# Second cross attention, selection: a text mask added by products over 128 rows of the array

## What is computed

```python
Q = (x_text @ Wq).reshape(Bb, Tt, H, DH)          # H = 4 heads, DH = 32
K = (x_vision @ Wk).reshape(Bb, Gg, H, DH)        # Gg = 4096
scores = jnp.einsum('bthd,bghd->bhtg', Q, K) / np.sqrt(DH).astype(np.float32)
scores = jnp.where(mask[:, None, None, :], scores, -jnp.inf)
topv, topi = jax.lax.top_k(scores, K_TOP)         # K_TOP = 32
probs = jax.nn.softmax(topv, axis=-1)
attn = jnp.zeros_like(scores).at[bi, hi, ti, topi].set(probs)
attn_mean = attn.mean(axis=1)
```

## Time and profile before

| | us |
|---|---|
| median of 3 runs | 2346.48 (2339.76 to 2350.98) |
| the profiled execution | 2345.02 |
| its span, first to last instruction | 2343.2 |
| TensorE busy, share of the span | 1861.1, 79% |
| VectorE busy | 1253.5, 53% |
| ScalarE busy | 1029.8, 44% |
| mean granted clock of TensorE | 0.854 |

### The profile page before, as it was taken

The page is one execution under the profiler, slowest core; times in us unless marked ns, Lnnn a source line. Parts: engine busy times, 40 slices in busy tenths (PEclk is TensorE's granted clock), DMA queues, the critical chain, the costliest instruction groups (busy, mean ns, idle before and its releaser), DMA issues.

```text
span 2343.2 us, 34857 instructions
## 1 busy us (share of the span) xinstructions
PE 1861.1 (79%) x13676; PEld 1136.0 (48%) x13676; DVE 1253.5 (53%) x3081; ACT 1029.8 (44%) x1381; POOL 769.4 (33%) x685
## 2 busy tenths in 40 slices
PE   5879999999999988886878687876877376766775
PEld 2434544454454445654664244544544355454553
DVE  5143332424233103556764859979789934636575
ACT  1357567657766871122212435455455211013452
POOL 6244334414432300001200457857678221310000
PEclk7989999999999999998886556777777698778887
DMA  6656557555553600002000011312211340000000
GB/s 139 126 102 117 114 117 120 119 116 107 114 118 88 114 39 1 2 2 92 27 2 12 14 55 48 88 50 60 82 48 55 106 152 1 0 1 1 1 5 14
DMA packets 78046, 150.27 MB, mean 64 GB/s; under 512 B 15464, under 2 KB 63144, under 8 KB 71464
## 3 DMA queue, kind: packets, MB, share of 16 engines
q1 hardware_dynamic: 64304, 102.06, 15.5%
q0 software_dynamic: 12768, 42.59, 11.8%
q10 hardware_dynamic: 792, 3.17, 0.3%
HBM read 93.85 MB, written 2.62 MB: 41 GB/s over the span
## 4 chain that ended last, share of the span: by engine, by line
PE 51%; DVE 25%; ACT 12%; issue 6%; DMA 4%; POOL 3%; DVEq 0%; ACTq 0%; POOLq 0%; SPq 0%
PE R L112 32%; PE B L112 17%; ACT P L571 6%; DVE PM L1700 6%; DVE CA L1658 4%; POOL KST L789 2%; DMA KST<-OV 2%; ACT PM L1585 2%; PE B L178 2%; DVE CA L1670 1%; DVE T L1672 1%; ACT PS L2253 1%; DVE RT L604 1%; DMA CT<-in_ctxT 1%; ACT RT L116 1%
## 5 line engine op out<-in xcount | busy, mean ns | idle before, releaser
L571 ACT ACTIVATE P<-R 128x1024 f32<-128x1024 f32 x512 | 506.9, 1026 | 217.6 <-PE R L112 182.6
L112 PE MATMUL R<-QS,KST 100*128 100x256 bf16 x2048 | 295.5, 276 | 61.8 <-ACT P L571 54.2
L112 PEld LDWEIGHTS R<-QS,KST 100*128 100x128 bf16 x2048 | 169.2, 98 | 225.5 <-ACT P L571 121.8
L116 ACT ACTIVATE SC<-R 128x1024 f32<-128x1024 f32 x128 | 129.6, 1024 | 240.3 <-PE R L112 129.5
L1658 DVE MAX8 CA<-SC 128x8 f32<-128x128 f32 x1024 | 203.2, 277 | 15.7 <-ACT SC L116 14.8
L200 POOL TENSOR_TENSOR LNrs<-LNve,pk_const 128x2 f32<-128x2 f32 x36 | 25.4, 705 | 521.5 <-DVE LNve L196 521.4
L112 PE MATMUL R<-OV,QT 32*128 32x512 f32 x512 | 190.9, 834 | 0.0
L1773 POOL TENSOR_TENSOR ACC<-ACC,PM 128x4096 f32<-128x4096 f32 x21 | 186.2, 8867 | 1.7
L1700 DVE SCALAR_TENSOR_TENSOR PM<-SC,T,PM 128x4096 f32<-128x4096 f32 x32 | 149.7, 4713 | 41.0 <-ACT AT L116 21.0
L789 POOL DMA_DIRECT2D KST<-OV x300 | 145.1, 492 | 73.8 <-PE R L112 56.4
L112 PE MATMUL R<-P,VP 128*32 128x256 f32 x2304 | 154.8, 385 | 1.0 <-ACT P L571 1.0
(11 more groups left out here) (364 smaller groups left out, 3407.3 us busy)
## 6 DMA issues: line engine op xcount, KB each, us to landing
KST<-OV POOLq DMA_DIRECT2D x276, 128.0 KB, 10.8
CT<-in_ctxP SPq DMA_DIRECT2D x40, 768.0 KB, 4.4
CN<-in_ctxn SPq DMA_DIRECT2D x64, 384.0 KB, 3.4
CT<-in_ctxT SPq DMA_DIRECT2D x64, 192.0 KB, 2.4
KST<-OV SPq DMA_DIRECT2D x84, 128.0 KB, 10.9
KST<-in_ctxP ACTq DMA_DIRECT2D x4, 768.0 KB, 9.1
QS<-x_q POOLq DMA_DIRECT2D x24, 128.0 KB, 5.5
pk_a<-in_pk_a SPq DMA_DIRECT2D x1, 3014.0 KB, 17.8
```

The source lines that it names most:

```text
L112: return e.matmul(o, l, r, start=st, stop=sp, skip_group_check=True)
L116: return e.activation(o, i, ACT.Copy)
L571: e.activation(P[(32 * p + k0) % 3][:, :], ring.at(("s", p, k0))[:, :], ACT.Exp).then_inc(*EX.up((p, k0)))
```

## The change

The mask is added by products over all 128 rows of the array: `ONB` is now zero but for its first row of ones, and `MRT` has the mask's row on partition 0 and zeros on the 127 others. The zeros are written once, by GpSimd, at the start of `stage_moe`. `ONB` takes two memsets and a wait between them. The mask's row goes to one partition, by one DMA in place of four. The number of products, what they write and their order remain.

```diff
@@ stage_moe, gpsimd
             def gpsimd(e):
+                e.memset(OV[:, NK:NK + NK // 2], 0.0)
                 for i in range(2):
                     ins = e.memset(LT[i][:, :], 0.0)
@@ stage_x1a, tensor, scores
                     for n in range(2):
-                        r = 32 * (2 * hp + n)
-                        mm(e, ps[:, n * 512:n * 512 + 512], ONB[r:r + 1, :], MRT[r:r + 1, cs], True, False)
+                        mm(e, ps[:, n * 512:n * 512 + 512], ONB[:, :], MRT[:, cs], True, False)
@@ stage_x1a, vector
                 e.memset(ON1[:, :], 1.0).then_inc(*QV.up())
-                e.memset(ONB[:, :], 1.0).then_inc(*QV.up("ones"))
+                e.memset(ONB[:, :], 0.0).then_inc(*QV.up())
+                e.wait_ge(*QV.now())
+                e.memset(ONB[0:1, :], 1.0).then_inc(*QV.up("ones"))
@@ stage_x1a, sync, mask_rows
-                    for h in range(4):
-                        e.dma_start(MRT[32 * h:32 * h + 1, :].rearrange("o (a k) -> o a k", k=128), MR[:, :]).then_inc(*MRD.up(b if h == 3 else None))
+                    e.dma_start(MRT[0:1, :].rearrange("o (a k) -> o a k", k=128), MR[:, :]).then_inc(*MRD.up(b))
```

## The result

| | before | changed |
|---|---|---|
| median of 4 runs, us | 2343.99 (2339.76 to 2350.98) | 2375.39 (2368.75 to 2381.61) |
| profiled execution, us | 2345.02 | 2371.99 |
| span, us | 2343.2 | 2370.2 |
| mean granted clock | 0.854 | 0.870 |

The changed kernel is slower: ratio 1.0131, 95% interval 1.0089 to 1.0172. The forecast was 2373 us.

A forecast was written before the change was run, and what follows sets the result against it. TensorE's chunks were taken to set the time in ten of 16 places, VectorE coming last in six. Batch 0 +10.0, eight places +12.8 and five +5 gave +27.8 us on 2345.0: 2373 us, range 2342 to 2402.

The forecast's parts named there:

- The second pass: Mask pair on TensorE: two 128-row products can't run side by side; +0.43 us a chunk at half clock, +0.21 at full.
- The change-over: Each chunk on TensorE: going from 128 rows to 32 and back costs 0.20 us, bounds 0 and 0.41.
- Places 0 and 1: First 16 chunks (a place: two heads, 128 queries, eight chunks): +2.4 us with the clock rising in place 1, +10.1 without.
- The sign named for it: Place 1: if the clock stays 0.50 behind the query product, the zero rows don't count.
- Place 2: Third place of batch 0: two chunks wait ready in the ring, six follow at half clock; +3.8 us.
- Place 3: Fourth place of batch 0, with the next batch's keys between chunks, at half clock; +3.8 us, chunks of about 6.6.
- The third rival: Full-row mask alone holds full clock from the first chunks; -21 us, 2324 us; place 3 chunks under 5 us; chance 0.18.
- That rows of zeros count for the clock: New masks on TensorE: full-row products count for raising the clock though 127 rows hold zeros.
- the rival of 2393 us: The clock doesn't react to zero rows in the new masks; +48 us, 2393 us; chance 0.22.
- The rest: Later places: eight waiting for ScalarE at 1.6 us each, +12.8; five with VectorE last at 1 each, +5.
- The smaller edits at nothing: GpSimd memset, ONB's second memset and wait, and single mask DMA: 0 us; DMA gain at most 1.8 us three times.

The follow-up runs named there:

- e2: Kernel before with each pair of one-row mask products issued twice, no change-over and no full rows; 2376.75 us, ratio 1.0132.
- e5: Kernel before with one product of 128 rows and a single column ahead of each one-row mask pair; 2368.66 us, ratio 1.0081.
- e3: Changed kernel with ones in place of zeros in the mask's 127 lower rows, weights there still zero; 2379.85 us, ratio 1.0143 to the kernel before.
- e1: Kernel before with mask products of 32 rows (one of mask, 31 of zeros) in each head's own strip, new memset included; 2348.28 us, ratio 1.0004.
- e7: Kernel before with idle 128-row products at the stage's start (36) and behind the second chunk of five places; 2328.28 us, ratio 0.9909.
- e8: Kernel before with 32-row masks in own strips, idle 128-row products at the stage's start, in five places and ahead of place 3; 2331.37 us, ratio 0.9895.
- e6: Kernel before with 36 idle 128-row products at the stage's start, while TensorE waits; one-row masks stay; 2347.72 us, ratio 0.9981.
- e9: Kernel before with 32-row masks in each head's own strip and 36 idle 128-row products at the stage's start; 2339.87 us, ratio 0.9943.

## Why the prediction was right, and where it was not

- **The second pass**: +0.43 and +0.21 us a chunk. Right: e2 measures 0.43 alone.
- **The change-over**: taken at 0.20, bounds 0 to 0.41. It was 0.41 at half clock (2.97 less 2.56) and 0.30 at full (1.59 less 1.08 and 0.21). The argument for the lower half, that the mask's weights are bf16 and quick, did not hold: e5 shows at most 0.23 for the change alone, and the rest lies between the score pair and the next mask, where the score pair's f32 weights may be the load that counts (argued, not shown). A chunk thus cost 0.84 or 0.51 where the sum had 0.63 or 0.41.
- **Places 0 and 1**: forecast +2.4 with the clock rising in place 1, +10.1 without. It did not rise: +12.5, which is 16 x 0.84 = 13.4 less a little that was hidden. The query product did not bring it up; this step failed. The sign named for it, that the zero rows don't count if place 1 stays at 0.50, misled as well: it stayed, and they count in place 3.
- **Place 2**: forecast +3.8, measured +4.9 (six chunks at 0.84 are 5.0). The size was off with the chunk's. That the whole of it counted was not in the rows: the selection of place 1, in which this section ends, was one of the six for which VectorE came last before. Its reserve was next to nothing, as e2 shows (+2.5 of 2.6).
- **Place 3**: forecast +3.8 at half clock, measured -9.8. This step failed too, in the other direction. The third rival had its test: if a chunk period in place 3 is under 5 us, the full-row mask holds the clock there. The masks at 1381.32, 1385.79 and 1389.61 us are 4.5 and 3.8 apart, with loads of the keys being waited for, just as that rival had it; but in places 0 to 2 it was wrong. The argument against it, that the 96-row keys had not raised the clock, was true of keys beside one-row masks and 32-row scores, and did not bear on keys beside full rows.
- **That rows of zeros count for the clock** was assumed; C bears it out (four traces with full-row masks against nine without), e3 adds that ones in the moving operand do no more than zeros, and the rival of 2393 us is out.
- **The rest**: +17.8 forecast for 13 places, +20.3 measured. Five places were said to have an unknown reserve; of these four lost it, as only one place now ends in VectorE's own check. The sum is near, but few places are: taken one by one, from 3 to 15, they moved by +3.5, +3.1, -0.8, -2.4, +3.5, +5.0, -2.8, -2.4, +3.4, +3.6, +4.1, +4.8 and -2.2 us, where 1.6 or 1 was forecast for each. Eight became 3.1 to 5.0 us longer, where six chunks without any earlier rise were to cost 2.9 (3.7 with the measured 0.84 and 0.51), and five became shorter.
- **The smaller edits at nothing**: e1 has the memset and the wait and 1.0004. The single mask DMA stands in no run by itself; its bound stays the forecast's, 1.8 us three times.

The total was right by luck: the errors of the four sections, +10.1, +1.1, -13.6 and +2.5 us, cancel to 0.1. A change-over sized at half and a rise expected in place 1 that did not come were paid back in place 3. The direction was no luck, and neither were the two costs behind it. e2 shows how large the bill would be without any help of the clock: 31 us for the second pass alone.

## What to carry to other kernels

Products on 32 rows that stand in different strips run side by side, and a product over all rows in their midst costs in two ways, both on the path here: its own serial pass (0.43 us a chunk at half clock) and the change-over with what follows it (0.41, of which at most 0.23 are the change itself). Where such work stands at half clock, as here, idle 128-row products in the gaps in which TensorE waits anyway can help (e7, e8: 1% faster; e6, with the first gap alone, nothing that can be measured); full rows in each step of the loop that sets the time cost more than they bring. And where a stage depends on when the clock rises, judge an edit by whole runs: gains of one section (14 us in e6) can be gone at the end.

## What the runs showed of the hardware

- Rows of zeros, or of ones, under zero weights, made no difference to the clock's rise: C is 44.9 and 44.1 us in the two.
- Work that left the clock at half in 42 us of being busy ran at full for a while once 128-row products had brought it up: with one-row masks for 17 us in e6 and 7 in e7, counted from the first mask, and with 32-row masks for the whole of places 0 and 1, 24 us, in e8 and e9. In all but e7 the transposes and the query product of place 1, of 128 rows, fall into that time.
- In the kernel before, four places had a first selecting pass of 5.4 to 7.6 us (4.48 is usual), in the changed one none: its 32 passes took 142.3 us in place of 149.7. Why is open: that the passes fall otherwise in time beside GpSimd's work is a guess, and no run tests it.
